# A decoder layer on one core: keys and exponentials turned by 32x32-block DMAs and VectorE transposes instead of TensorE

## The chip, the core and the metric

The kernel runs on one NeuronCore of a Trainium2 chip. The metric is the device time of one execution in microseconds; a comparison takes the median of several executions. The kernel before takes 1527.0 us (three runs: 1527.0, 1528.57, 1527.0).

## The reference

One post-norm decoder layer on 4 sequences of 512 tokens with 512 features: gated slot attention with 16 heads, a cross attention on a context of 4 x 512 x 256, and a quantized feed-forward of width 2048. Cut to what matters here:

```python
q, k = heads(x @ Wq, 64), heads(x @ Wk, 64)
v, s = heads(x @ Wv, 64), clip(heads(x @ Ws, 64), -32, 32)
z = cumlogsumexp(s, axis=time)
# hk_t = hk_(t-1) * exp(z_(t-1) - z_t) + k_t outer exp(s_t - z_t) ; ok_t = q_t @ hk_t
# hv_t = hv_(t-1) * exp(z_(t-1) - z_t) + exp(s_t - z_t) outer v_t ; o_t = softmax(ok_t) @ hv_t
o = rmsnorm(o) * g_norm_weight * silu(x @ Wg)
x = layernorm(x + o @ Wo)
x = layernorm(x + x @ softmax((ctx @ xWq + bq) @ (ctx @ xWk + bk).T))
x = layernorm(x + h_bitlinear(silu(bitlinear(x, w_gate)) * bitlinear(x, w_up), w_down))
```

The recurrences over time are computed in four chunks of 128 tokens. A chunk's state is the sum over its tokens of k outer exp(s); this sum is a matmul that needs k and exp(s) with **tokens on the partitions**, while the projections deliver them with features on the partitions and tokens along the row. So both have to be transposed, and that is what the change is about.

## The kernel before, in words

**Steps.** `PAIRS` lists 32 pairs (pair of heads, sequence). One attention step works on one pair: two heads side by side on 128 partitions, 512 tokens along the row. Step n runs the tail of pair n (states, sums, ok, softmax, weights, values), the projections of pair n+1 (`q`, `k`, `s`, `vg0` to `vg3`) and the output projection of pair n-1 (`turn_o`, `y`). All large matmuls are three passes (high x high, low x high, high x low) at lines 453, 456 and 459.

**The order of the work** is written out by hand in the tuples `ALONE` (steps 0 to 20) and `STEP` (from step 21); every engine walks the same list and picks its share, so a place in the tuple is a place in each engine's queue. Stages in `OF_NEXT` belong to pair n+1. The stage `tern` is a piece of preparing the ternary feed-forward weights: its first 24 tasks take sums of absolute values (ScalarE), the last 24 round (ScalarE) and clip and store (GpSimd, lines 1385 and 1388, semaphore `w3_made`). From step 22 on, cross attention is put between the stages by `PLACES` (one table per sequence: stage name and place number), then come a seam (`SEAM`) and the feed-forward in units of 128 features (`UNIT`). `HOLD` says for how many later requests a PSUM bank is taken to be busy, and so which bank comes next.

**The two transposes.** In the stage `keys` TensorE transposes KT (keys, 3 chunks of 128x128, line 500) and ET (exponentials, 4 chunks, line 504) against the identity into two PSUM banks; ScalarE copies them to Kt and Et (lines 814 and 819); the next step's first stage, `states`, multiplies Kt by Et (line 522). KT is written by ScalarE in stage `k` (line 799) and ET in stage `s` (line 802, the exponential). Kt and Et have one buffer each; Et of pair n is also read by `ok` (line 541) and `sums` (line 529) of step n.

**The DMA queue of SyncE (SP)** issues the weights: `pieces` is their order, two raw buffers `RAW` take turns, and before each piece SP waits until the buffer's former content was used (`left_raw`: for weights the low half made by GpSimd, line 1377; for feed-forward weights `w3_abs` or `w3_made`). Nothing overtakes on that queue. It also loads x into Y (line 1468) ahead of the first feed-forward weights.

**Head and tail.** SP issues the first pieces one after the other: x, Wq, x, x, x, Wk. At the end, the 16 `down` products of the last token tile go into one bank of 512 columns (line 717); VectorE adds it to Y (line 1312), takes moments (line 1315), GpSimd takes the root (line 1423), VectorE normalises (line 1322), and SP stores.

Of the kernel before, what the change touches and what calls it, by code (L numbers as in the profile page):

```python
# [35 lines left out]

class Queue:
# [5 lines left out]
    def wait_ge(self, sem, value):  # L43
        if value > self.passed.get(sem.name, 0):
# [6 lines left out]
         "y", "scores", "weights", "vg2", "load_x", "values", "keys", "tern", "vg3")  # L51
STEP = ("states", "q", "k", "tern", "load_x", "ok", "sums", "turn_o", "s", "turn_ok", "vg0", "turn_w", "tern", "vg1",
        "y", "vg2", "scores", "weights", "load_x", "values", "keys", "tern", "vg3")
OF_NEXT = ("q", "k", "s", "vg0", "vg1", "vg2", "vg3", "scores", "keys")


def step_order(n, tasks):

    terns = loads = 0
    for stage in ALONE if n < 21 else STEP:  # L60
        m = n + 1 if stage in OF_NEXT else n - 1 if stage in ("turn_o", "y") else n
        if stage == "tern":
            terns += 1
            if n and terns in ((2,) if n + 1 in LAST else (1, 2, 3)):
                for t in tasks[:1]:
                    yield stage, t
                del tasks[:1]
        elif stage == "load_x":
            loads += 1
            if n == 0:  # L70
                yield stage, loads + 1
        elif 0 <= m < STEPS:
            yield stage, m
# [26 lines left out]

PLACED = [stage for stage in STEP if stage not in ("scores", "sums", "load_x", "tern")]


def attention_order():

    for stage in OF_NEXT:
        yield stage, 0
    tasks = list(range(52))
    for n in range(STEPS - 1):
# [6 lines left out]
SEAM = (("states", 31), ("turn_o", 30), ("sums", 31), ("ok", 31), ("y", 30), ("turn_ok", 31), ("unit", 0), ("unit",  # L116
        1), ("turn_w", 31), ("unit", 2), ("weights", 31), ("unit", 3), ("values", 31), ("unit", 4), ("turn_o", 31),
# [6 lines left out]
def seam_order():  # L124

    for p, item in enumerate(SEAM):
        if item and item[0] == "unit":
            yield from ffn_place(item[1])
        elif item:
# [6 lines left out]
    dict(ctx=396, centre=402, n1=406, qk=407, qk_out=409, x101=414, x101_out=415, energy=417, energy_out=418,  # L136
         x123=419, att_scale=419, x123_out=420, att01=422, att01_out=424, att23=425, att23_out=426, xm0=430,
# [6 lines left out]
    dict(ctx=474, centre=474, n1=476, qk=477, qk_out=478, x101=479, x101_out=481, energy=481, energy_out=482,  # L144
         att_scale=483, att01=486, x123=487, x123_out=488, att01_out=488, att23=488, att23_out=489, xm0=491,
         xm0_out=492, xm1=493, xm1_out=494, xm2=495, xm2_out=496, xm3=497, xm3_out=498, x_round0=513, x_made0=514,
         x_round1=514, x_made1=515, x_turned=516, x_turned_out=517),
    dict(ctx=499, qk=502, qk_out=504, centre=518, n1=520, energy=522, energy_out=523, x101=524, att_scale=524,
# [19 lines left out]
def beside(place):  # L168
# [6 lines left out]
        38), ("low", 2), ("turn_q_out", 32), ("had2_out", 24), ("round", 29), ("high", 2), ("gs", 0), ("add", 35),  # L175
        ("had1", 4), ("normal", 37), ("turn_q", 31), ("had2", 23), ("down", 33), ("silu", 0))
# [4 lines left out]
HOLD = (("o", 12), ("en", 11), ("y", 7), ("vg", 9), ("xm", 11), ("gate", 7), ("up", 8), ("h1", 7), ("h2", 8), ("down",  # L181
        11), ("hq", 6), ("xt", 11), ("q", 5), ("k", 9), ("s", 9), ("sc", 13), ("wt", 7), ("ok", 12), ("okt", 8), ("w",
        6), ("ot", 10), ("kt", 4), ("et", 6), ("hk", 7), ("hv", 9), ("att", 12), ("x1", 11), ("qk", 11), ("spread",
# [27 lines left out]
vec_made hk_zero  # L211
x_hi x_lo_v x_lo_g w_hi w_lo_v w_lo_g wo_scaled w3_abs w3_sum w3_total w3_mean w3_round w3_clip w3_made
proj_q proj_k proj_s proj_vg q_evac k_evac s_clip e_exp v_evac g_tanh u_made
z_scan z_recip k_turned e_turned kt_evac et_evac scores a_masked hk_mm hv_mm hk_evac hv_evac hk_add hv_add
# [10 lines left out]
def build(nc, x, xT, Wq, Wk, Wv, Wg, Ws, Wo, gw, cT, xWqT, xbq, xWkT, xbk, wgT, wuT, wdT, cst, out):  # L225
    with ExitStack() as top:
# [143 lines left out]

        weight_no = {key: i + 1 for i, key in enumerate(key for key, _, _ in pieces if key[0] not in "xF")}
# [55 lines left out]
        def tensor(engine):  # L427
# [62 lines left out]
            def attend(stage, n):  # L490
                par = n % 2
                if stage == "keys":
                    bk = take(("kt", n), (S["kt_evac"], n + 1))
                    be = take(("et", n), (S["et_evac"], n + 1))
# [6 lines left out]
                    mm.then_inc(S["k_turned"], 1)  # L501
# [3 lines left out]
                    mm.then_inc(S["e_turned"], 1)  # L505
# [11 lines left out]
                elif stage == "states":  # L517
                    bh = take(("hk", n), (S["hk_evac"], n + 1), (S["hk_add"], 2 * n + 2))
                    pe.wait_ge(S["kt_evac"], n + 1)
                    pe.wait_ge(S["et_evac"], n + 1)  # L520
# [182 lines left out]
            def ffn_tile(stage, i):  # L703
# [8 lines left out]
                elif stage == "down":  # L712
                    bk = take(("down", i), (S["ffn_add"], i + 1))
                    pe.wait_ge(S["w3_in2"], 16 * 4)
                    for j in range(16):
                        pe.wait_ge(S[f"hq_evac{j // 8}"], i + 1)
                        mm = engine.matmul(bk[:], HT[:, j, :], WD[:, j, :], start=j == 0, stop=j == 15)  # L717
                    mm.then_inc(S["down"], 1)
# [30 lines left out]
        def scalar(engine):  # L749
# [19 lines left out]
            def ternary(t):  # L769
# [10 lines left out]
                elif what == "made":  # L780
# [4 lines left out]
                    act.wait_ge(S["vec_made"], 2)  # L785
# [3 lines left out]
            def attention(stage, n):  # L789
# [5 lines left out]
                elif stage == "k":  # L795
                    act.wait_ge(S["proj_k"], n + 1)
                    act.wait_ge(S["scores"], 2 * n)
                    act.wait_ge(S["e_turned"], n)
# [787 lines left out]
```

## Time and profile before

| | |
|---|---|
| median of three runs | 1527.0 us |
| the profiled execution, its own time | 1525.28 us |
| its span, first to last instruction | 1523.4 us |
| TensorE busy (PE) | 1488.2 us, 98% |
| VectorE busy (DVE) | 1032.0 us, 68% |
| ScalarE busy (ACT) | 653.9 us, 43% |
| GpSimd busy (POOL) | 432.0 us, 28% |
| DMA packets | 108016, 121.17 MB |

The table is read with two cautions. A busy TensorE is a row of matmuls that overlap: what one costs is the distance from its start to the start of the next, not its duration. And the busy share of another engine is an average over stages in which it is idle and stages in which everything waits for it.

### The profile page before, as it was taken

What the parts mean: (1) busy time and instruction counts of PE and PEld (TensorE: products, weight loads), DVE (VectorE), ACT (ScalarE), POOL (GpSimd) and SP (SyncE); (2) the same over time, 40 slices, a digit from 0 to 9 for tenths busy, and PEclk for the clock granted to TensorE, in tenths of its full rate; (3) what the DMA queues carried; (4) which work ended last, traced back from release to release, by engine and by line L of the source; (5) the groups of instructions that cost most, each with busy time, mean ns of one, the idle gap of its engine ahead of it and who ended that gap; (6) DMA issues with size and microseconds to landing.
All of it is one profiled execution on the core that took longest, in us unless ns stands there. A gap on an engine that the chain in (4) does not pass through costs nothing.

```text
span 1523.4 us, 24179 instructions
## 1 busy us (share of the span) xinstructions
PE 1488.2 (98%) x9536; PEld 1207.2 (79%) x9570; DVE 1032.0 (68%) x1990; ACT 653.9 (43%) x1249; POOL 432.0 (28%) x282
## 2 busy tenths in 40 slices
PE   8999999999999999999999999999999898999998
PEld 6888888888888888888888888878878655666675
DVE  5666665566556666665666577777787776877788
ACT  5333333333323333333443333424243357677775
POOL 0211011110214344433454423122331333333320
PEclk9999999999999999999999999999999999999999
DMA  4511111120102121222223211101110315344552
GB/s 154 180 52 67 42 49 56 56 66 33 63 15 79 62 88 65 83 70 70 84 80 101 87 28 54 49 22 42 52 41 26 111 70 176 122 132 136 155 170 93
DMA packets 108016, 121.17 MB, mean 80 GB/s; under 512 B 5376, under 2 KB 75136, under 8 KB 107904
## 3 DMA queue, kind: packets, MB, share of 16 engines
q1 hardware_dynamic: 104448, 113.33, 23.5%
q10 hardware_dynamic: 3456, 6.29, 1.1%
q8 instruction: 77, 1.26, 0.3%
q14 instruction: 35, 0.29, 0.1%
HBM read 92.34 MB, written 27.26 MB: 79 GB/s over the span
## 4 chain that ended last, share of the span: by engine, by line
PE 92%; DVE 5%; issue 2%; ACT 1%; DMA 0%; POOL 0%; POOLq 0%; SPq 0%; DVEq 0%; ACTq 0%
PE bank L453 19%; PE bank L459 18%; PE bank L456 18%; PE bank L682 6%; PE bank L579 4%; PE bank L697 4%; PE bank L717 3%; PE bank L541 2%; PE bank L514 2%; PE bank L587 2%; PE bank L565 2%; PE bank L536 1%; PE bank L522 1%; PE bank L529 1%; PE bank L573 1%
## 5 line engine op out<-in xcount | busy, mean ns | idle before, releaser
L453 PE MATMUL bank<-Wh,X 128*128 128x512 f32 x512 | 210.5, 411 | 0.1
L459 PE MATMUL bank<-Wh,X 128*128 128x512 f32 x512 | 201.0, 393 | 0.0
L456 PE MATMUL bank<-Wl,X 128*128 128x512 f32 x512 | 199.8, 390 | 0.0
L808 ACT ACTIVATE V<-bank 128x256 f32<-128x256 f32 x128 | 49.0, 383 | 315.5 <-PE bank L459 315.5
L453 PE MATMUL bank<-X,Wh 128*128 128x512 f32 x384 | 157.2, 409 | 7.6 <-ACT Wh L763 5.9
L1395 POOL TENSOR_TENSOR sm<-sm,half 128x8 f32<-128x8 f32 x32 | 52.8, 1649 | 387.3 <-DVE sm L1109 387.2
L1377 POOL TENSOR_TENSOR Wl<-RAW,Wh 128x512 fp32r<-128x512 f32 (+1 forms) x65 | 112.3, 1737 | 136.5 <-ACT Wh L763 136.5
L456 PE MATMUL bank<-X,Wh 128*128 128x512 f32 x384 | 151.0, 393 | 0.0
L459 PE MATMUL bank<-X,Wl 128*128 128x512 f32 x384 | 150.8, 393 | 0.0
L1418 POOL TENSOR_TENSOR LO<-M,HI 128x512 fp32r<-128x512 f32 x64 | 81.8, 1278 | 165.5 <-PE bank L691 106.0
L682 PE MATMUL bank<-XT,W 128*128 128x512 bf16 x492 | 118.1, 381 | 4.2 <-ACT XI L881 2.3
L1045 DVE SCALAR_TENSOR_TENSOR U<-U,bank 128x256 f32<-128x256 f32 x128 | 51.6, 404 | 100.9 <-ACT U L810 100.9
L459 PEld LDWEIGHTS bank<-Wh,X 128*128 128x128 f32 x512 | 96.1, 188 | 21.6
L453 PEld LDWEIGHTS bank<-Wh,X 128*128 128x128 f32 x512 | 96.3, 188 | 19.3 <-ACT Kt L814 0.4
L456 PEld LDWEIGHTS bank<-Wl,X 128*128 128x128 f32 x512 | 96.6, 189 | 17.2
L1043 DVE RECIPROCAL ZT<-ZT 128x512 f32<-128x512 f32 x32 | 107.3, 3353 | 1.1
L1385 POOL TENSOR_SCALAR RAW<-RAW 128x1024 f32<-128x1024 f32 x24 | 87.1, 3629 | 62.7 <-ACT RAW L786 62.2
L453 PE MATMUL bank<-Woh,OTh 128*128 128x512 f32 x256 | 99.8, 390 | 0.0
L456 PE MATMUL bank<-Wol,OTh 128*128 128x512 f32 x256 | 99.6, 389 | 0.0
L459 PE MATMUL bank<-Woh,OTl 128*128 128x512 f32 x256 | 99.6, 389 | 0.0
L1080 DVE TENSOR_TENSOR OKM<-bank,ZT 128x512 f32<-128x512 f32 x32 | 22.1, 691 | 112.0 <-PE bank L541 111.9
L682 PEld LDWEIGHTS bank<-XT,W 128*128 128x128 bf16 x512 | 48.8, 98 | 56.5 <-issue 8.5
(207 smaller groups left out, 3312.3 us busy)
## 6 DMA issues: line engine op xcount, KB each, us to landing
z_scratch<-EV SPq DMA_DIRECT2D x64, 256.0 KB, 2.0
Z<-z_scratch SPq DMA_DIRECT2D x16, 1024.0 KB, 5.9
RAW<-wgT SPq DMA_DIRECT2D x16, 512.0 KB, 3.9
RAW<-wuT SPq DMA_DIRECT2D x16, 512.0 KB, 3.8
RAW<-wdT SPq DMA_DIRECT2D x16, 512.0 KB, 3.6
RAW<-Wo SPq DMA_DIRECT2D x14, 512.0 KB, 3.6
RAW<-Wv SPq DMA_DIRECT2D x26, 256.0 KB, 2.9
RAW<-Wg SPq DMA_DIRECT2D x26, 256.0 KB, 3.4
```

The source lines that it names most:

```text
L453: engine.matmul(o, lh(c), rh(c), start=c == 0, stop=False)
L456: engine.matmul(o, lh(c), rl(c), start=False, stop=False)
L459: last = engine.matmul(o, ll(c), rh(c), start=False, stop=c == n - 1)
L579: mm = engine.matmul(bo[h][:, 128 * i:128 * i + 128], AM[:, h, i, :], V[:, par, i, 128 * h:128 * h + 128], start=False, stop=i == 3)
L682: mm = engine.matmul(bk[:], w[:, c, 128 * j:128 * j + 128], XT[b % 3][:, c, :], start=c == 0, stop=c == 3)
L697: mm = engine.matmul(bh[:, 128 * c:128 * c + 128], Z[:, i % 2, 4 * q + c, :], C[:, 4, :], start=True, stop=True)
L1043: engine.reciprocal(ZT[:], ZT[:]).then_inc(S["z_recip"], 1)
L1045: engine.scalar_tensor_tensor(u, u, 1.0, bank("vg", n, i)[:, 256:512], ALU.add, ALU.mult).then_inc(S["u_made"], 1)
L1377: engine.tensor_tensor(lo, r, hi, ALU.subtract).then_inc(S["w_lo_g"], 1)
L1385: engine.tensor_scalar(r, r, MAGIC - 1.0, MAGIC + 1.0, ALU.max, ALU.min).then_inc(S["w3_clip"], 1)
L1395: engine.tensor_tensor(smv[:, 4, :], smv[:, 3, :], half[:, 0:8], ALU.pow).then_inc(S["o_rstd"], 1)
L1418: engine.tensor_tensor(LO[:, n % 2, :], M[n % 3], HI[:, n % 3, :], ALU.subtract).then_inc(S["h_lo"], 1)
```

## The change

1. From pair 1 on, KT and ET are transposed without TensorE. SP issues 16 DMAs for each: DMA (a, b) moves the 32x32 blocks at partitions 32a of every chunk to partitions 32b of Kt (or Et), block columns 32a. So the blocks stand at their transposed places, and one VectorE `transpose` over the whole tile then turns each block inside, in place. The new stages `turn_k` (after `vg1`) and `turn_e` (after `vg2` or `weights`) hold the two VectorE instructions. The stage `keys` remains for pair 0 alone, now ahead of `scores`.
2. SP issues a send after the pieces whose buffer is freed earlier in the order, and before those that are freed later.
3. `load_x` of the last two sequences: one in step 0 and one in step 1 (before: both in step 0), without the first `tern` of step 1. The loads of Y are issued behind the second send of exponentials.
4. Head: the load of Wq is issued by ScalarE. Tail: the last `down` product is made in two halves of 256 columns, in two banks; add and moments follow per half.
5. Tables: `HOLD`, some places of `PLACES` (sequences 0, 2 and 3), the order in `SEAM` (`ok` ahead of `sums`, `unit 1` behind `turn_w`) and in `UNIT` (`round` last, `high` ahead of `had2_out`).

```diff
-         "y", "scores", "weights", "vg2", "load_x", "values", "keys", "tern", "vg3")
+         "turn_k", "y", "scores", "weights", "vg2", "turn_e", "values", "tern", "vg3")
...
-    dict(ctx=474, centre=474, n1=476, qk=477, qk_out=478, x101=479, x101_out=481, energy=481, energy_out=482,
+    dict(ctx=474, centre=474, qk=474, qk_out=475, n1=476, x101=479, x101_out=481, energy=481, energy_out=482,
...
+        def sent(n):
+            return 16 * 16 * n
...
                 if stage == "keys":
+                    if n:
+                        return
...
+            def turn(stage, n):
+                if stage == "turn_k":
+                    dve.wait_ge(S["kt_in"], sent(n))
+                    k = Kt[:].rearrange("p i n -> p (i n)")
+                    engine.transpose(k, k).then_inc(S["kt_made"], 1)
+                else:
+                    dve.wait_ge(S["et_in"], sent(n))
+                    e = Et[:].rearrange("p i n -> p (i n)")
+                    engine.transpose(e, e).then_inc(S["et_made"], 1)
...
+            def send(stage, n):
+                if stage == "k":
+                    sp.wait_ge(S["k_evac"], n + 1)
+                    sp.wait_ge(S["hk_mm"], n)
+                    src, to, done = KT[:, 0:384].rearrange("p (i b c) -> p i b c", i=3, b=4), Kt, S["kt_in"]
+                else:
+                    sp.wait_ge(S["e_exp"], n + 1)
+                    sp.wait_ge(S["ok_sum"], n)
+                    sp.wait_ge(S["hv_mm"], n)
+                    src, to, done = ET[:, n % 2, :].rearrange("p (i b c) -> p i b c", i=4, b=4), Et, S["et_in"]
+                for a in range(4):
+                    for b in range(4):
+                        engine.dma_start(to[32 * b:32 * b + 32, :, 32 * a:32 * a + 32],
+                                         src[32 * a:32 * a + 32, :, b, :]).then_inc(done, 16)
...
+                buffer = where if where in (0, 1) else None
+                until = max(until, freed.get(held.get(buffer), -1))
+                while sends and sends[0][0] < until:
+                    send(*sends.pop(0)[1:])
...
+                        halves = (bk, take(("down", 16), (S["ffn_add"], 17)))
+                        for js, cols, bh in [(js, cols, bh) for js in (range(8), range(8, 16))
+                                             for cols, bh in zip(COLUMNS, halves)]:
```

**Order on TensorE in step 17, around `values` and `vg3`.** V, AM are the values and the masked weights, C holds the identity, Wh and X the weights and x of `vg3`. Before:

```order
L459 MATMUL bank5<-Wh,X 128x512
L579 MATMUL bank3<-V,AM 128x128 [waits a2_masked]
L579 MATMUL bank3<-V,AM 128x128 x3
L579 MATMUL bank6<-V,AM 128x128 [waits a2_masked]
L579 MATMUL bank6<-V,AM 128x128 x3
L500 MATMUL bank4<-C,KT 128x128 [waits e_exp,y_add]
L500 MATMUL bank4<-C,KT 128x128 x2
L504 MATMUL bank7<-C,ET 128x128 x4
L453 MATMUL bank1<-Wh,X 128x512
L456 MATMUL bank1<-Wl,X 128x512
```

and with the change:

```order
L468 MATMUL bank4<-Wh,X 128x512
L591 MATMUL bank1<-V,AM 128x128 [waits a2_masked]
L591 MATMUL bank1<-V,AM 128x128 x3
L591 MATMUL bank2<-V,AM 128x128 [waits a2_masked]
L591 MATMUL bank2<-V,AM 128x128 x3
L462 MATMUL bank6<-Wh,X 128x512 [waits y_add]
L465 MATMUL bank6<-Wl,X 128x512
```

The seven transposes are gone, and nothing stands in their place.

**Order on VectorE in the same step, from the end of `vg1` to `values`.** ZT is the running sum, U the gate, Y the output, AM the masked weights, OG the squares. Before:

```order
L1043 RECIPROCAL ZT<-ZT 128x512 [waits z_scan]
L1045 SCALAR_TENSOR_TENSOR U<-U,bank6 128x256 [waits g_tanh]
L1136 TENSOR_TENSOR Y<-Y,bank1 128x512 [waits y_add,y_mm]
L1136 TENSOR_TENSOR Y<-Y,bank3 128x512 [waits y_mm]
L1136 TENSOR_TENSOR Y<-Y,bank5 128x512 [waits y_mm]
L1136 TENSOR_TENSOR Y<-Y,bank4 128x512 [waits y_mm]
L1102 TENSOR_TENSOR AM<-bank7,C 128x512 [waits weights]
L1102 TENSOR_TENSOR AM<-bank1,C 128x512 [waits weights]
L1045 SCALAR_TENSOR_TENSOR U<-U,bank5 128x256 [waits g_tanh]
L1106 TENSOR_REDUCE sm<-OG 128x2x4 [waits o_square]
```

and with the change:

```order
L1081 RECIPROCAL ZT<-ZT 128x512 [waits z_scan]
L1083 SCALAR_TENSOR_TENSOR U<-U,bank1 128x256 [waits g_tanh]
L1055 STREAM_TRANSPOSE Kt<-Kt 128x384 [waits kt_in]
L1174 TENSOR_TENSOR Y<-Y,bank0 128x512 [waits y_add,y_mm]
L1174 TENSOR_TENSOR Y<-Y,bank2 128x512 [waits y_mm]
L1174 TENSOR_TENSOR Y<-Y,bank4 128x512 [waits y_mm]
L1174 TENSOR_TENSOR Y<-Y,bank6 128x512 [waits y_mm]
L1140 TENSOR_TENSOR AM<-bank7,C 128x512 [waits weights]
L1140 TENSOR_TENSOR AM<-bank0,C 128x512 [waits weights]
L1083 SCALAR_TENSOR_TENSOR U<-U,bank4 128x256 [waits g_tanh]
L1059 STREAM_TRANSPOSE Et<-Et 128x512 [waits et_in]
L1144 TENSOR_REDUCE sm<-OG 128x2x4 [waits o_square]
```

Two transposes are added, each with a wait for DMAs: one ahead of the four additions to Y, one ahead of the sum of squares.

**Order on SP's queue around steps 16 and 17.** RAW<-wuT is a piece of feed-forward weights. Before:

```order
L1505 DMA RAW<-wuT 128x1024 [waits w3_made] x3
L1499 DMA RAW<-Wo 128x2x512 [waits w3_made]
L1505 DMA RAW<-wuT 128x1024 [waits w3_made]
L1505 DMA RAW<-wuT 128x1024 [waits w_lo_g]
L1505 DMA RAW<-wuT 128x1024 [waits w3_made] x2
```

and with the change, from the sends of exponentials in step 16 to those in step 17:

```order
L1523 DMA Et<-ET 32x4x32 [waits hv_mm,ok_sum,e_exp]
L1523 DMA Et<-ET 32x4x32 x15
L1594 DMA RAW<-wuT 128x1024 [waits w3_made]
L1594 DMA RAW<-wuT 128x1024 [waits w_lo_g]
L1594 DMA RAW<-wuT 128x1024 [waits w3_made] x2
L1523 DMA Kt<-KT 32x3x32 [waits hk_mm,k_evac]
L1523 DMA Kt<-KT 32x3x32 x15
L1523 DMA Et<-ET 32x4x32 [waits hv_mm,ok_sum,e_exp]
L1523 DMA Et<-ET 32x4x32 x15
```

The 16 sends of keys stand behind a piece that waits for GpSimd, and the 16 sends of exponentials behind those.

## Rows read from the trace of the kernel before

**Rows 1.** The page: part 1, part 4.

```profile
PE 1488.2 (98%) x9536; PEld 1207.2 (79%) x9570; DVE 1032.0 (68%) x1990; ACT 653.9 (43%) x1249; POOL 432.0 (28%) x282
PE 92%; DVE 5%; issue 2%; ACT 1%; DMA 0%; POOL 0%; POOLq 0%; SPq 0%; DVEq 0%; ACTq 0%
```

**Rows 2.** Timeline of TensorE, one step: start, us, engine, line, operation, count.

```profile
616.93 1.95 PE L579 MATMUL bank<-V,AM 128*128 128x128 f32 x16
618.72 0.49 PE L500 MATMUL bank<-C,KT 128*128 128x128 f32 x3
619.04 0.60 PE L504 MATMUL bank<-C,ET 128*128 128x128 f32 x4
619.40 0.47 PE L453 MATMUL bank<-Wh,X 128*128 128x512 f32 x1
...
622.25 0.83 PE L522 MATMUL bank<-Et,Kt 128*128 128x128 f32 x6
...
657.38 0.83 PE L522 MATMUL bank<-Et,Kt 128*128 128x128 f32 x6
```

**Rows 3.** Waits of TensorE: for whom, us in total, times, longest.

```profile
PE bank L587 <- DVE OG L1118: 4.0, 1, 4.0
...
PE bank L579 <- DVE AM L1102: 2.1, 1, 2.1
...
PE bank L565 <- DVE U L1045: 1.9, 1, 1.9
...
PE bank L453 <- DVE AM L1053: 1.1, 1, 1.1
```

**Rows 4.** Windows: us, busy of PE, PEld, DVE, ACT, POOL, PEclk, DMA, GB/s.

```profile
1020.00:1030.00 10.00, 7.34 (x65) 6.56 (x64) 8.61 (x23) 4.67 (x7) 5.02 (x3) 0.83 0.09 28
...
1200.00:1220.00 20.00, 14.71 (x97) 10.08 (x97) 12.98 (x26) 8.31 (x14) 7.26 (x5) 0.94 0.00 1
```

**Rows 5.** Timeline of ScalarE, the step of rows 2.

```profile
629.13 0.58 ACT L799 ACTIVATE KT<-bank 128x512 f32<-128x512 f32 x1
...
634.67 0.63 ACT L802 ACTIVATE ET<-ET 128x512 f32<-128x512 f32 x1 [3.43 <-DVE ET L1031]
```

**Rows 6.** Timeline of GpSimd, the step of rows 2.

```profile
633.01 1.04 POOL L1388 TENSOR_SCALAR BW<-RAW 128x1024 bf16<-128x1024 f32 x1
```

**Rows 7.** Timeline of SP's queue: DMAs issued back to back.

```profile
42.94 3.82 SPq L1468 DMA_DIRECT2D Y<-x  x4
...
798.58 0.47 SPq L1474 DMA_DIRECT2D XI<-xWkT  x1
799.09 0.47 SPq L1455 DMA_DIRECT2D CTX<-cT  x1
```

**Rows 8.** The page, parts 3 and 6: queue, packets, MB, share; issues, median us to landing.

```profile
q1 hardware_dynamic: 104448, 113.33, 23.5%
...
z_scratch<-EV SPq DMA_DIRECT2D x64, 256.0 KB, 2.0
```

**Rows 9.** Timeline of VectorE, the step of rows 2.

```profile
645.68 2.47 DVE L1136 TENSOR_TENSOR Y<-Y,bank 128x512 f32<-128x512 f32 x4
648.64 1.29 DVE L1102 TENSOR_TENSOR AM<-bank,C 128x512 f32<-128x512 f32 x2 [0.50 <-PE bank L565]
652.96 0.42 DVE L1045 SCALAR_TENSOR_TENSOR U<-U,bank 128x256 f32<-128x256 f32 x1 [3.02 <-ACT U L810]
654.68 1.22 DVE L1106 TENSOR_REDUCE sm<-OG 128x8 f32<-128x1024 f32 x1 [1.30 <-ACT OG L840]
```

**Rows 10.** The chain that ended last, around 1005 to 1026 us: start, us, what.

```profile
1014.65 3.35 DVE ZT L1043
```

**Rows 11.** Timeline: TensorE before the first step, VectorE in the tail.

```profile
29.69 0.91 PE L522 MATMUL bank<-Et,Kt 128*128 128x128 f32 x6 [0.78 <-ACT Et L819]
...
1517.85 0.75 DVE L1312 SCALAR_TENSOR_TENSOR Y<-bank,fs,Y 128x512 f32<-128x512 f32 x1 [1.78 <-PE bank L717]
1518.64 0.69 DVE L1315 BATCH_NORM_STATS2 st<-Y 128x6 f32<-128x512 f32 x1
```

More of the change, by code:

```diff
@@ L50 @@
 ALONE = ("states", "q", "tern", "k", "load_x", "ok", "sums", "s", "turn_ok", "turn_o", "vg0", "tern", "turn_w", "vg1",
-         "y", "scores", "weights", "vg2", "load_x", "values", "keys", "tern", "vg3")
-STEP = ("states", "q", "k", "tern", "load_x", "ok", "sums", "turn_o", "s", "turn_ok", "vg0", "turn_w", "tern", "vg1",
-        "y", "vg2", "scores", "weights", "load_x", "values", "keys", "tern", "vg3")
-OF_NEXT = ("q", "k", "s", "vg0", "vg1", "vg2", "vg3", "scores", "keys")
+         "turn_k", "y", "scores", "weights", "vg2", "turn_e", "values", "tern", "vg3")
+STEP = ("states", "q", "tern", "k", "load_x", "ok", "sums", "turn_o", "s", "turn_ok", "vg0", "tern", "turn_w", "vg1",
+        "y", "turn_k", "vg2", "scores", "weights", "turn_e", "values", "tern", "vg3")
+OF_NEXT = ("q", "k", "s", "vg0", "vg1", "vg2", "vg3", "keys", "scores", "turn_k", "turn_e")
 def step_order(n, tasks):
@@ L69, in step_order @@
             loads += 1
-            if n == 0:
-                yield stage, loads + 1
+            if n < 2 and loads == 1:
+                yield stage, n + 2
         elif 0 <= m < STEPS:
@@ L97, in raw_tasks @@
     yield STEPS - 1, ("WO", LOADS - 1)
-PLACED = [stage for stage in STEP if stage not in ("scores", "sums", "load_x", "tern")]
+PLACED = [stage for stage in STEP if stage not in ("scores", "sums", "load_x", "tern", "turn_k")]
 def attention_order():
-    for stage in OF_NEXT:
+    for stage in OF_NEXT[:9]:
         yield stage, 0
@@ L1327, in attention @@
                     project(stage, n)
+                elif stage in ("turn_k", "turn_e"):
+                    turn(stage, n)
                 else:
@@ L1484, in sync @@
                     placed.add(2)
+                if key == ("Q", 0):
+                    held[where] = key
+                    continue
                 buffer = {"am0": "am", "am1": "am", "og0": "og", "og1": "og"}.get(where, where)
@@ L1508, in sync @@
                                      wd[kind][:, :, 128 * hp:128 * hp + 128]).then_inc(done, 16)
+            for _, stage, n in sends:
+                send(stage, n)
             sp.wait_ge(S["ctx_lo_g"], 2)
```

122 lines of the change are left out of this document (78 added, 44 removed).

## The prediction

> **What bounds the kernel now.** I read the page's engine shares first, then the chain that ended last, then the waits of TensorE, then timelines of one step. TensorE is busy 98% of the span and holds 92% of the chain [rows 1]; so a TensorE instruction removed shortens the kernel by its start-to-start distance, where nothing new is waited for. One step runs from 622.25 to 657.38, 35.13 us [rows 2], with no TensorE wait inside it. What TensorE does wait for is a handful of single places [rows 3]; 4.0, 2.1 and 1.9 us of it lie in the stretch where cross attention and the seam are mixed in, and behind two of them the granted clock falls for a while [rows 4]. VectorE's 5% of the chain [rows 1] lies there too: around 1005 to 1026 us VectorE itself sets the pace, for example with a 3.35 us reciprocal [rows 10].
>
> **The change part by part.**
>
> *Transposes on TensorE.* The last value product starts a run at 616.93; the first transpose follows at 618.72, and `vg3` begins at 619.40 [rows 2]. Seven transposes cost 619.40 - 618.72 = 0.68 us, though their durations add up to more (they overlap). They go in 31 of 32 steps: 31 x 0.68 = **21.1 us**. The two ScalarE copies behind them go as well, worth nothing (ScalarE is 43% busy [rows 1]).
>
> *Keys, in their place.* In the step of rows 2 KT is ready at 629.13 + 0.58 = 629.71 [rows 5]. But the sends stand behind a piece that waits for GpSimd, which is done at 633.01 + 1.04 = 634.05 [rows 6]; with that piece's own issue (0.47 us [rows 7]) the sends begin at 634.5. No row shows a 32x32-block DMA. Nearest are plain DMAs issued back to back: 798.58 to 799.09, 0.51 us apart [rows 7]; the dearest in a row are the 1 MB loads of Y, 3.82 / 4 = 0.96 us each [rows 7]. A block DMA moves 12 or 16 KB, so I take 0.51 and keep 0.96 for the range. 16 x 0.51 = 8.2 us: issued by 642.7, landed by 644.7 with the 2.0 us of the 256 KB transfers [rows 8]. VectorE comes to `turn_k` just ahead of the additions to Y, at 645.68 [rows 9]: in time by 1 us.
>
> *Exponentials.* ET is ready at 634.67 + 0.63 = 635.3 [rows 5], earlier than the queue: issue 642.7 to 650.9, landed 652.9. VectorE comes to `turn_e` after the gate of `vg2`, 652.96 + 0.42 = 653.4 [rows 9]; in time by half a microsecond. TensorE needs the result at 657.38 - 0.68 = 656.7 [rows 2].
>
> *The VectorE transposes.* No row shows one. A 128x256 operation takes 0.42 us, a 128x512 addition 2.47 / 4 = 0.62 us [rows 9], and the dearest 128x512 operation 3.35 us [rows 10]. I take 0.55 (384 columns) and 0.65 (512 columns), near the plain operations. `turn_k` shifts the additions to Y from 645.68 and ends them at about 648.7, when VectorE waits for the weights anyway (0.50 us of idle, masks from 648.64); `turn_e` falls into 1.30 us of idle ahead of 654.68 [rows 9]. The masked weights are done by 650.0, `values` starts at about 652. So in plain steps both cost nothing; the cover is VectorE's idle time. At 3.35 us each they would cost 3 us a step.
>
> The Trainium skill (VectorE: DVE Perf Modes, The three transpose paths) gives 311 ns for a 128x128 VectorE transpose in bf16, an estimate of 0.93 and 1.24 us for 3 and 4 chunks; the sum below would be 0.8 us longer by it.
>
> *Where VectorE sets the pace.* Two chains lead to the waits of 2.1 and 1.9 us [rows 3]. There TensorE's 0.68 us only lengthens the wait, and `turn_k` (0.55) lies in the chain: 2 x 1.23 = **+2.5 us**. Below: 0; above: one new wait of the longest kind.
>
> *SP's queue.* The sends take 16.3 of 35 us. The weight loads behind them are late by 8 us each time, but two raw buffers and a whole step stand between load and use; I cost that at nothing. If the cover fails it shows as ScalarE waiting for a DMA.
>
> *Order of x loads, keys ahead of scores.* The wait of 1.1 us in step 0 [rows 3] comes from a VectorE mask behind the squares, with two x loads rounded just before; with one of them in the next step it goes: **-1.1**. Before the first step TensorE waits 0.78 us for the copy of Et [rows 11]; `scores` now stands between: **-0.8**. Late next are the sends of pair 1, with 10 us to spare.
>
> *Head and tail.* Wq's load is issued one place (0.47 us [rows 7]) earlier: between 0 and -0.5, taken **-0.2**. At the end, addition and moments of 0.75 and 0.69 us over 512 columns [rows 11] become halves, the first beside TensorE; 0.42 us for 256 columns [rows 9] leaves 0.6 to gain, less a little for twice the matmuls: **-0.5**, bounds 0 and -0.7.
>
> *Tables* (`PLACES`, `HOLD`, `SEAM`, `UNIT`): unknown sign. Best case, the three waits of rows 3 that lie there go (8.0 us) with their clock losses, (1 - 0.83) x 10 = 1.7 and (1 - 0.94) x 20 = 1.2 us [rows 4]: -10.9. Worst case, two more like the longest, 2 x (4.0 + 1.7) = +11.4. Taken 0, as nothing favours a side.
>
> *Sum*, against the profiled execution's own 1525.28 us: 1525.28 - 21.1 + 2.5 - 1.1 - 0.8 - 0.2 - 0.5 = 1504.1. The median of the runs is 1527.0, 1.7 above that execution; so **1505.8 us**.
>
> **The rivals.**
>
> *Slower: the queue sets the step.* The last block must land and be turned by 656.7. From 634.5, with 2.0 for landing and 0.65 for the turn, 32 issues have 19.5 us: 0.61 us each. Beyond it every step whose sends wait behind GpSimd pays 32 times the excess; by the order these are 5 steps with three rounding tasks and 9 that change weights ahead of the long cross steps, 14 in all. At 0.70 us it is 14 x 2.9 = 41 us: 1547. It decides at about 0.66 us, where the loss eats the 21 us. For it: the 0.96 of Y's loads. Against it: those are 1 MB each and fill the queues; every smaller one is at about 0.5.
>
> *Slower: the packets set it.* 128-byte runs mean 16 x 96 packets for keys and 16 x 128 for exponentials, 96 and 128 per DMA engine. The mean packet took 0.235 x 16 x 1523.4 / 104448 = 0.055 us [rows 8], at some 1085 bytes: 5.3 and 7.0 us, under the 8.2 of the issues. If each took double, 0.11, the two need 24.6 us instead of 19.5: 14 x 5.1 = 71 us, 1577. The Trainium skill has such a rule (DMA: Bandwidth & Descriptors, Specifications): below 512 bytes the engine reads, modifies and writes. No row here shows what that costs; a transfer between SBUF places with such runs is not in this trace.
>
> *New waits in the cross stretch*, the worst case of the tables: 1505.8 + 11.4 = 1517. For it: VectorE is the fullest there and gets two more instructions a step, each with a wait that holds all behind it.
>
> *The old waits go*, the best case: 1505.8 - 10.9 = 1495. For it: two PSUM banks are free in each step.
>
> *No change*: the saved 0.68 us is only waited elsewhere, if landings come late by just that: 1526. Against it: TensorE has no wait in the plain steps.
>
> **How the numbers follow.** Forecast 0.62 (its own range 1500 to 1511, from the bounds of head, tail, VectorE and half a new wait), old waits go 0.08, new waits 0.14, no change 0.05, the queue 0.08, the packets 0.03. Faster by more than 0.2% (3 us, about what a measurement of this kernel can tell): 0.62 + 0.08 + 0.14 = 0.84; within 0.2%: 0.05; slower: 0.11. The range takes in both cases of the tables with a margin of 2 us for a run against a run: 1493 to 1519; left out are 0.16.
>
> **What would show it.** Right: steps of 34.45 us in the plain part; seven transposes left in all on TensorE; issues of block DMAs about 0.5 us apart; VectorE transposes of 0.4 to 0.7 us with no TensorE wait at the `states` products; the waits in step 0 and before the first step gone. Wrong: a wait of `states` for VectorE's transposes, repeated every step (the queue or the packets); VectorE waiting long for the DMAs at `turn_k`, then TensorE for masks; ScalarE waiting for weight loads; or more idle time between 1000 and 1260 us than the 8 us of rows 3.

## The result and the profile after

The changed kernel takes **1557.3 us** (median of four runs, 1555.3 to 1557.7) against 1527.0: a ratio of 1.020, interval 1.019 to 1.021. The forecast was 1505.8 with a range of 1493 to 1519; the change made the kernel slower, in the way of the rival "the queue sets the step". All rows of the changed kernel below come from its profiled execution of 1557.0 us, with a span of 1555.0.

The page of the changed kernel, part 1 and the two rows of part 4, to be held against [rows 1]:

```profile
PE 1487.1 (96%) x9369; PEld 1194.8 (77%) x9369; DVE 1066.3 (69%) x2054; ACT 625.1 (40%) x1187; POOL 432.4 (28%) x282
PE 57%; SPq 20%; POOL 8%; DVE 5%; DMA 4%; issue 4%; ACT 2%; ACTq 0%; POOLq 0%; DVEq 0%
SPq L1523 19%; PE bank L462 10%; PE bank L468 10%; PE bank L465 10%; PE bank L694 6%; PE bank L709 4%; PE bank L730 3%; POOL RAW L1437 3%; POOL Wl L1429 3%; PE bank L591 2%; DMA Et<-ET 1%; PE bank L577 1%; DMA RAW<-Wk 1%; PE bank L553 1%; PE bank L526 1%
```

TensorE held 92% of the chain that ended last and now holds 57%. SP's queue, at 0% before, holds 20%, nearly all of it line 1523, the block DMAs. GpSimd's 8% is mostly the rounding (L1437) and the low halves of the weights (L1429), behind which the sends stand. Step 16, from 595.03 to 631.80, is the one ahead of the step that the prediction worked through (17), and VectorE comes to the keys at the same place in it, 23.5 us after its start against 23.4. The timeline of SP's queue in it (start, time from the first issue's start to the last one's end, engine, line, operation, count):

```profile
607.67 0.38 SPq L1588 DMA_DIRECT2D RAW<-Wo  x1
608.15 10.21 SPq L1523 DMA_DIRECT2D Kt<-KT  x16
618.47 11.21 SPq L1523 DMA_DIRECT2D Et<-ET  x16
629.73 11.18 SPq L1594 DMA_DIRECT2D RAW<-wuT  x3
```

The sends begin 13.1 us after the step's start at 595.03, 0.9 us later than the prediction put them in its step. But 16 issues take 10.21 and 11.21 us, **0.64 and 0.70 us each, not 0.51**: the last leaves at 629.68, not 16.3 but 21.5 us after the first. The page's part 6 gives the landings (count, KB each, median us from issue to landing), 1.8 and 1.9 us, near the 2.0 of [rows 8]:

```profile
Kt<-KT SPq DMA_DIRECT2D x496, 12.0 KB, 1.8
Et<-ET SPq DMA_DIRECT2D x496, 16.0 KB, 1.9
```

VectorE in the same step (in brackets the idle time before an instruction, and who ended it), where [rows 9] had no such waits:

```profile
619.59 0.58 DVE L1055 STREAM_TRANSPOSE Kt<-Kt 128x384 f32<-128x384 f32 x1 [1.05 <-DMA Kt<-KT]
620.10 2.44 DVE L1174 TENSOR_TENSOR Y<-Y,bank 128x512 f32<-128x512 f32 x4
...
630.94 0.71 DVE L1059 STREAM_TRANSPOSE Et<-Et 128x512 f32<-128x512 f32 x1 [3.53 <-DMA Et<-ET]
```

and TensorE, its only two waits in that step, to be held against [rows 2], where there was none:

```profile
595.03 0.83 PE L534 MATMUL bank<-Et,Kt 128*128 128x128 f32 x6
...
621.49 1.16 PE L577 MATMUL bank<-WT,ET 64*128 64x128 f32 x16 [0.99 <-DVE Y L1174]
...
631.80 0.91 PE L534 MATMUL bank<-Et,Kt 128*128 128x128 f32 x6 [1.02 <-DVE Et L1059]
```

The keys come 1.05 us late and hold the four additions to Y, which hold the PSUM bank that the weights want; the exponentials come 3.53 us late and hold the states. The step takes 36.77 us instead of 35.13.

In step 17 itself, from 631.80, a second loss shows. Before, its first rounding task began 0.54 us after the step's start at 622.25:

```profile
622.79 3.63 POOL L1385 TENSOR_SCALAR RAW<-RAW 128x1024 f32<-128x1024 f32 x1
```

With the change the load that this task needs leaves SP only behind the sends of step 16, at 629.73. ScalarE waits 5.78 us for it, and everything behind it is late:

```profile
634.46 1.24 ACT L810 ACTIVATE RAW<-RAW,half,ws 128x1024 f32<-128x1024 f32 x1 [5.78 <-DMA RAW<-wuT]
635.79 3.63 POOL L1437 TENSOR_SCALAR RAW<-RAW 128x1024 f32<-128x1024 f32 x1 [1.09 <-ACT RAW L810]
647.52 10.27 SPq L1523 DMA_DIRECT2D Kt<-KT  x16
```

The rounding begins 3.99 us into the step, the sends 15.7 us into it instead of the predicted 12.3, and the step takes 39.78 us. So the queue's delay comes round: late sends make the next loads late, these the rounding, and this the next sends.

The waits of TensorE over the whole run (for whom, us, times, longest) show the same two at the head of the list, ahead of everything in [rows 3]:

```profile
PE bank L534 <- DVE Et L1059: 22.2, 10, 4.9
PE bank L577 <- DVE Y L1174: 15.2, 10, 3.5
PE bank L462 <- ACT Wh L787: 6.2, 1, 6.2
```

The waits are not all that was lost: behind the longer ones the granted clock falls. At the start of step 1 TensorE waits 3.82 us. The sends of pair 1 begin at 37.15, 7.1 us into step 0, and their last issue ends at 60.02; 1.2 us of that are two loads of x between keys and exponentials. Step 0 had lasted 28.89 us before, so the exponentials come too late. And then:

```profile
62.16 0.91 PE L534 MATMUL bank<-Et,Kt 128*128 128x128 f32 x6 [3.82 <-DVE Et L1059]
...
64.25 0.63 PE L465 MATMUL bank<-X,Wh 128*128 128x512 f32 x1
64.68 0.63 PE L468 MATMUL bank<-X,Wl 128*128 128x512 f32 x1
...
66.77 0.40 PE L465 MATMUL bank<-X,Wh 128*128 128x512 f32 x1
```

The matmuls are 0.43 us apart there, against 0.23 in other steps: the lower of the two levels (1.2 GHz), until about 66.4. A window over the weight rounding, 440 to 940 us (columns as in [rows 4], `xN` are counts), before:

```profile
440.00:940.00 500.00, 499.47 (x3287) 425.02 (x3286) 316.24 (x577) 185.35 (x368) 209.46 (x106) 1.00 0.23 71
```

and after:

```profile
440.00:940.00 500.00, 466.53 (x2939) 389.83 (x2938) 301.12 (x549) 160.66 (x313) 199.41 (x98) 0.97 0.30 80
```

Before, TensorE is busy throughout at full clock; after, it idles and the mean clock is 0.97.

Step times, from the starts of the first `states` product of each step on TensorE's timeline; the second column has each step between the starts of 3 and 11, the third is (start of step 25 - start of step 11) / 14:

| kernel | steps 3 to 11 | mean of steps 11 to 25 | whole run, us |
|---|---|---|---|
| before | 35.13 | 35.15 | 1527.0 |
| changed | 34.3 to 34.6 | 37.84 | 1557.3 |

So the transposes' saving is there where no rounding task stands ahead of the sends, and lost where the rounding tasks and changes of weights do, in the 14 steps from 11 to 25.

### The profile page after: what moved, and what is told of

The parts are those of the page before. It is cut to its first block, busy times and chain, and to the rows that moved or that the text cites. A ratio compares the mean times of both kernels' runs of the same rounds, so it can differ in the third digit from the quotient of the medians.

```text
span 1555.0 us, 24857 instructions
## 1 busy us (share of the span) xinstructions
PE 1487.1 (96%) x9369; PEld 1194.8 (77%) x9369; DVE 1066.3 (69%) x2054; ACT 625.1 (40%) x1187; POOL 432.4 (28%) x282
## 2 busy tenths in 40 slices
DMA packets 234998, 135.49 MB, mean 87 GB/s; under 512 B 132352, under 2 KB 202112, under 8 KB 234880
## 4 chain that ended last, share of the span: by engine, by line
PE 57%; SPq 20%; POOL 8%; DVE 5%; DMA 4%; issue 4%; ACT 2%; ACTq 0%; POOLq 0%; DVEq 0%
SPq L1523 19%; PE bank L462 10%; PE bank L468 10%; PE bank L465 10%; PE bank L694 6%; PE bank L709 4%; PE bank L730 3%; POOL RAW L1437 3%; POOL Wl L1429 3%; PE bank L591 2%; DMA Et<-ET 1%; PE bank L577 1%; DMA RAW<-Wk 1%; PE bank L553 1%; PE bank L526 1%
## 5 line engine op out<-in xcount | busy, mean ns | idle before, releaser
L462 PE MATMUL bank<-X,Wh 128*128 128x512 f32 x384 | 160.1, 417 | 7.6 <-ACT Wh L787 6.2
L465 PE MATMUL bank<-X,Wh 128*128 128x512 f32 x384 | 153.7, 400 | 0.0
L1429 POOL TENSOR_TENSOR Wl<-RAW,Wh 128x512 fp32r<-128x512 f32 (+1 forms) x65 | 112.2, 1736 | 105.4 <-ACT Wh L787 105.4
L694 PE MATMUL bank<-XT,W 128*128 128x512 bf16 x512 | 123.5, 385 | 4.7 <-ACT XI L906 2.4
L462 PEld LDWEIGHTS bank<-Wh,X 128*128 128x128 f32 x512 | 96.8, 189 | 19.5 <-issue 0.6
L1437 POOL TENSOR_SCALAR RAW<-RAW 128x1024 f32<-128x1024 f32 x24 | 87.1, 3630 | 63.5 <-ACT RAW L810 63.1
L462 PEld LDWEIGHTS bank<-X,Wh 128*128 128x128 f32 x384 | 74.6, 194 | 25.8 <-ACT Wh L787 6.2
```

The lines of the kernel that those rows point to most:

```text
L462: engine.matmul(o, lh(c), rh(c), start=c == 0, stop=False)
L465: engine.matmul(o, lh(c), rl(c), start=False, stop=False)
L694: mm = engine.matmul(bk[:], w[:, c, 128 * j:128 * j + 128], XT[b % 3][:, c, :], start=c == 0, stop=c == 3)
L1429: engine.tensor_tensor(lo, r, hi, ALU.subtract).then_inc(S["w_lo_g"], 1)
L1437: engine.tensor_scalar(r, r, MAGIC - 1.0, MAGIC + 1.0, ALU.max, ALU.min).then_inc(S["w3_clip"], 1)
```

## The experiments

The page's row names and line numbers are those of each kernel; ratios are to the kernel before, run on the same chip at the same time.

**1. The price of an issue alone.** A kernel without the layer: groups of 16 DMAs of 32x3x32 blocks and of other shapes, one after the other.

> Nothing of the layer is computed here: groups of 16 DMAs issued back to back, each group after the one before has landed; the output is a copy of x. Queue theory (each issue from SP has a price of its own that hardly depends on what it moves): the groups of 32x3x32 and 32x4x32 blocks show 0.62 to 0.70 us per issue, as in the changed kernel, and a third of the packets (32x1x32) does not bring it under 0.55; landing about 2 us after the last issue. Packet theory (the 128-byte runs keep the DMA engines busy and hold the queue back): 32x1x32 falls to 0.45 or less, and 64- and 128-partition blocks of the same runs rise to 1.2 us or more. A third outcome: the price hangs on the form (32 partitions, SBUF as source); then 128-partition or plain 512-column transfers show 0.5 and the HBM source too. ScalarE's queue: the same as SP's by both theories; GpSimd's: open, 0.5 to 2 us.

Timeline rows of the DMA-issuing queues, each a group of 16; `t_k` blocks within SBUF, `t_plain` 32 rows of 512 columns within SBUF, `t_h2s` from HBM (blocks, then plain rows), `t_act` and `t_pool` blocks from the two other queues, `t_both` from two at once:

```profile
6.18 10.34 SPq L43 DMA_DIRECT2D t_k<-src  x16
...
76.12 10.07 SPq L43 DMA_DIRECT2D t_plain<-src  x16
87.64 7.43 SPq L43 DMA_DIRECT2D t_h2s<-x  x16
96.46 7.29 SPq L43 DMA_DIRECT2D t_h2s<-x  x16
105.40 10.39 ACTq L43 DMA_DIRECT2D t_act<-src  x16
...
128.95 8.76 POOL L43 DMA_DIRECT2D t_pool<-src  x16 [128.51 <-DMA t_act<-src]
138.93 10.68 SPq L43 DMA_DIRECT2D t_both_sp<-src  x16
138.93 10.39 ACTq L43 DMA_DIRECT2D t_both_act<-src  x16
```

10.34 / 16 = 0.65 us for a block DMA, 0.63 for a plain one within SBUF, 0.46 for either shape from HBM. The groups of other shapes in between took 10.0 to 11.0 us; one of them moves 384 runs of 128 bytes with each DMA, four times those of a block, in 10.74. Block shape, run length and packets hardly matter; both ends in SBUF does. The rows on which I had put my 0.51 [rows 7] are all loads from HBM.

**2. Fewer packets, same issues.** Only the first chunk of each tile moves, so a third and a quarter of the bytes; keys and exponentials are otherwise left as they were.

```diff
-                        engine.dma_start(to[32 * b:32 * b + 32, :, 32 * a:32 * a + 32],
-                                         src[32 * a:32 * a + 32, :, b, :]).then_inc(done, 16)
+                        engine.dma_start(to[32 * b:32 * b + 32, 0:1, 32 * a:32 * a + 32],
+                                         src[32 * a:32 * a + 32, 0:1, b, :]).then_inc(done, 16)
```

> The sends move only the first of the 3 (or 4) chunks, so Kt and Et are stale in the other chunks: the same 32 DMAs a step with 32 packets each in place of 96 and 128. Queue theory: issues stay at 0.55 to 0.69 us, the made steps stay late: 1535 to 1560 us. Packet theory: the landings come early and the kernel falls to 1500 to 1512 us.

One execution: 1547.6 us, span 1545.7, steps 11 to 25 at a mean of 37.35 us. In step 16 the two groups of 16 issues take 10.02 and 10.55 us. With 32 packets in place of 96 and 128 per DMA most of the loss is still there: not the packets.

**3. Sends ahead of the gated pieces.** A piece that a rounding task frees counts as freed two places later, one freed by the exponentials' weights one place later. So the sends of keys overtake the piece of the step's first rounding task, and those of exponentials the other.

```diff
-    freed["F", n // 27, n % 27 // 8, n % 27 % 8] = place
+    freed["F", n // 27, n % 27 // 8, n % 27 % 8] = place + 2
...
-    freed[key] = place
+    freed[key] = place + (key[0] == "S")
```

> Only SP's order differs: the sends of keys go ahead of the piece that waits for the step's first rounding task, and the sends of exponentials ahead of the piece that waits for the low half of S. Queue theory: in steps with three rounding tasks the sends begin at 7.5 us after the step's start in place of 12.3, and with 32 issues of 0.66 us the last block is turned 4 us earlier, just in time, so those steps return to about 34.4 us; steps that change weights stay about 1 to 2 us late. Together 1510 to 1535 us. Theory that the sends themselves (packets, or VectorE's waits wherever they stand) cost it: 1550 us or more.

1546.5 us, ratio 1.013 (1.0115 to 1.0145), outside both expectations. Most steps fell to between 34.4 and 36.2 us, but two took 49.6 and 48.3. In the first of them, SP's queue,

```profile
741.23 10.21 SPq L1523 DMA_DIRECT2D Kt<-KT  x16
751.55 11.67 SPq L1523 DMA_DIRECT2D Et<-ET  x16
763.26 0.59 SPq L1588 DMA_DIRECT2D RAW<-Wo  x1
```

and VectorE:

```profile
767.44 0.75 DVE L1030 TENSOR_SCALAR RAW<-RAW,gwc 128x1024 f32<-128x1024 f32 x1 [11.81 <-DMA RAW<-Wo]
```

The load of Wo now leaves behind 22 us of sends, VectorE waits 11.81 us for it in front of the masks, and TensorE 9.49 us for those. The queue is simply full at that place: whatever stands first there makes the other late.

**4. Keys by DMA, exponentials on TensorE.** `turn_e` becomes four TensorE transposes and a ScalarE copy behind the values; 16 sends a step remain.

> Keys go by DMA and VectorE, exponentials by TensorE and ScalarE as before: 16 issues a step in place of 32, four transposes back on TensorE (0.36 us a step). Queue theory: nothing is late any more, steps of 35.13 - 0.32 = 34.8 us: 1514 to 1522 us. If the loss came from the tables (places, banks, seam) and not from the queue: 1540 us or more.

1526.6 us, ratio 1.0001 (0.9991 to 1.001), slower than the 1514 to 1522 expected. Steps 2 to 11 take 34.81 us, a saving of 0.32 in each, as expected; steps 11 to 25 have a mean of 35.66, with one of 40.05. What remains is the wait at the weights for the additions to Y (7.7 us in 6 waits). The keys' own 16 issues still take 10.3 and 11.3 us in the two steps from 562.28 and 599.57, VectorE waits up to 3.46 us for them, and the saving is given back.

**5. Half the block DMAs.** Half of the blocks keep old contents; the count that VectorE waits for is halved with them.

```diff
-            return 16 * 16 * n
+            return 16 * 8 * n
...
-                    for b in range(4):
+                    for b in range(2):
```

> Only 8 of the 16 block DMAs of every tile are issued (b = 0 and 1), so half of Kt and Et keep old contents; all else as changed, both VectorE transposes included. Theory 'the issues on SP': 16 issues of 0.64 to 0.69 us are 10.7 us a step in place of 21.3, so from 634.5 the keys land at about 641.6 and the exponentials at about 647, both before VectorE comes to them; steps 12 to 25 fall to 34.3 to 34.8 us, the half-clock stretches behind the waits go, and the 38 us lost there and the 9 us not gained come back: 1505 to 1515. Rival 'the VectorE transposes and the moved orders': they are all still there, so the time stays above 1540.

**1498.9 us**, ratio 0.983 (0.981 to 0.984); steps 11 to 25 at 34.49; 6 us better than the best expected. SP's queue in step 16 issues 8 and 8 in 5.1 us each:

```profile
587.46 5.08 SPq L1523 DMA_DIRECT2D Kt<-KT  x8
592.65 5.09 SPq L1523 DMA_DIRECT2D Et<-ET  x8
```

All else of the change, VectorE's transposes included, is in this kernel. Halving the issues takes away 58 us. It halves the bytes and packets too, but run 2 took more of those away for 10 us: the loss lies in the issues.

**6. The same work with 10 issues.** One DMA writes each tile into a scratch in HBM, four read the blocks back to their transposed places.

```diff
+                blocks = z.rearrange("i (a p) (b c) -> b p i a c", a=4, b=4).rearrange("b p i a c -> b p (i a) c")
+                for b in range(4):
+                    engine.dma_start(to[32 * b:32 * b + 32].rearrange("p i (a c) -> p (i a) c", a=4),
+                                     blocks[b]).then_inc(done, 16)
...
+                engine.dma_start(zt[n % 2, 1].rearrange("i p n -> p i n"),
+                                 ET[:, n % 2, :].rearrange("p (i n) -> p i n", i=4)).then_inc(S["et_in"], 16)
```

> All of the computation; each tile goes through a scratch in HBM: one DMA writes it (SBUF as source), four read the blocks back to their transposed places (HBM as source). 10 issues a step in place of 32: 2 x 0.65 + 8 x 0.46 = 5.0 us, and each write has to land (about 2 us) before its reads. From 634.5 in the step of rows 2: writes issued by 635.9, keys read from about 637.5 and landed by 641.5, exponentials landed by 643.5; both before VectorE comes (645.7 and 653.4). Theory 'the issues on SP': plain steps of 34.3 to 34.8 us throughout, 1500 to 1515. Rival 'the way over DMA itself' (short runs, landing, VectorE's transposes, moved orders): the steps stay at 36 us or more behind the rounding tasks, above 1530.

**1498.7 us** (1498.5 to 1499.5), ratio 0.982 (0.981 to 0.984): the whole computation, faster than both kernels. SP's queue in step 17, which starts at 610.06:

```profile
623.07 0.43 SPq L1521 DMA_DIRECT2D t_scratch<-KT  x1
623.54 0.49 SPq L1525 DMA_DIRECT2D t_scratch<-ET  x1
627.46 1.86 SPq L1515 DMA_DIRECT2D Kt<-t_scratch  x4
629.43 2.00 SPq L1515 DMA_DIRECT2D Et<-t_scratch  x4
```

From first issue to last it is 8.4 us in place of 21.0 in step 17 of the changed kernel (21.5 in its step 16), the landing of the write (623.07 to 627.46) included, and the issues cost 0.43 to 0.50 each. The write lands later than I said (a median of 4.1 and 3.8 us, not 2), which the step has room for. The waits of TensorE and the window of the rounding stretch:

```profile
PE bank L463 <- ACT Wh L788: 6.3, 1, 6.3
...
PE bank L578 <- DVE Y L1175: 1.7, 2, 1.2
```

```profile
440.00:940.00 500.00, 498.25 (x3247) 422.01 (x3246) 338.18 (x625) 178.79 (x354) 216.98 (x110) 1.00 0.37 100
```

No wait for the states is left, two of 1.2 us or less for the additions, and the clock is at 1.00. The DMA share rose to 0.37 from 0.30, with more bytes and more packets than the changed kernel has (149.63 against 135.49 MB, 251857 against 234998 packets): more traffic, less time.

**7. The same, with `turn_k` next to `turn_e`,** behind the additions to Y:

```diff
-         "turn_k", "y", "scores", "weights", "vg2", "turn_e", "values", "tern", "vg3")
+         "y", "scores", "weights", "vg2", "turn_k", "turn_e", "values", "tern", "vg3")
...
```

> As the version over HBM, and the VectorE transpose of the keys stands next to that of the exponentials, behind the additions to Y and the gate, where TensorE's states first need it. If late keys ahead of the additions to Y still cost something there (the issue theory says little, since the keys are in time), this is 1 to 4 us faster than the version before; if nothing is late, the same within 1.5 us; the rival (VectorE's two transposes in a row late in the step delay the masks and the sum of squares) would make it 2 us or more slower.

1497.9 us (1497.6 to 1500.9), ratio 0.982: not to be told from run 6 in time. In the trace nearly every step from 2 to 25 takes 34.34 us, that of 35.79 in run 6 too.

**8. Everything else of the change.** Keys and exponentials back on TensorE, no sends; head, tail, x loads and tables as changed.

> No sends and no VectorE transposes: TensorE turns keys and exponentials for all pairs behind the values, with two ScalarE copies, as in the kernel before; head, tail, x loads, loads of Y and all tables as in the changed kernel. Theory 'the issues on SP': all of the loss lies in the sends, so this is the kernel before with the small terms of head, tail and step 0 (-1.8): 1520 to 1528, with steps of 35.1 us. Rival 'the moved orders': if the tables or the x loads cost the time, it stays at 1535 or more.

1527.0 us, ratio 1.0012 (1.0002 to 1.0021), steps of 35.13. The rest of the change together is worth nothing, within 0.2%.

**9. The block DMAs, with `turn_k` next to `turn_e`.** The edit of run 7 in the changed kernel.

> The changed kernel with one move: VectorE's transpose of the keys stands next to that of the exponentials, behind the additions to Y. Theory 'late keys hold the additions': TensorE's waits at the weights for the additions (15.2 us in 10 waits) go, with the half-clock stretches behind them: 1530 to 1545. Rival 'only the last block counts': the exponentials leave behind the keys on the same queue, so what the additions no longer wait for is waited for at the states, in the same steps: 1550 to 1560.

1555.4 us, ratio 1.019 (1.017 to 1.020). The wait at the weights went (15.2 us), and that at the states rose from 22.2 to 35.9 us in 14 waits. The rival I had set up is right: the order on VectorE decides where TensorE waits, not how long.

**10. Run 9 with the sends ahead of the first rounding task's piece,** the weights' loads left ahead of the exponentials (the first edit of run 3 alone).

> As the run before, and the sends of keys and exponentials stand ahead of the piece that the first rounding task frees (the piece counts as freed two places later), while the pieces freed by the exponentials' weights stay ahead of the sends of exponentials. The sends of keys then begin at about 630 in place of 634.5 in the step of rows 2: 26.7 us up to 656.7 for 32 issues of 0.64 to 0.69 (21.3 us) and 2.5 for landing and turn. Theory 'the queue in order': the steps fall to 34.3 to 35.6 and the two stretches of 48 to 50 us of the first such trial (a load of Wo late behind the sends) don't come: 1508 to 1525. Rival: what the sends gain, the weight loads behind them lose, on the same queue: 1540 or more.

1533.4 us, ratio 1.004 (1.003 to 1.006), between the two theories: the two long steps are gone, the mean of steps 11 to 25 is 36.25 us, and TensorE still waits 19.4 us at the states. Order alone gives back 22 of the 57 us between runs 9 and 7: where the sends start counts beside what they take.

**11. Two queues.** GpSimd issues the exponentials, SP the keys.

> The 16 sends of exponentials are issued by GpSimd at its place of that stage, the 16 sends of keys by SP as before; the same 32 DMAs, bytes and packets. Theory 'the issues on one queue': SP's share is 10.3 us a step, GpSimd's 16 x 0.55 = 8.8 us beside it, both done in time: 1500 to 1520, with GpSimd's rounding tasks some 9 us later in each step. Rival 'the DMA engines or the packets': the same transfers take as long from two queues, 1545 or more.

1610.8 us, ratio 1.056: a miss, and no test of what it was made for. GpSimd's timeline in one step:

```profile
700.75 1.74 POOL L1496 DMA_DIRECT2D Et<-ET  x3 [2.63 <-ACT ET L829]
705.48 1.64 POOL L1496 DMA_DIRECT2D Et<-ET  x3 [2.99 <-issue]
708.70 1.64 POOL L1496 DMA_DIRECT2D Et<-ET  x3 [1.57 <-issue]
...
718.00 0.55 POOL L1496 DMA_DIRECT2D Et<-ET  x1 [1.45 <-issue]
718.57 1.29 POOL L1429 TENSOR_TENSOR Wl<-RAW,Wh 128x512 fp32r<-128x512 f32 x1
719.95 3.62 POOL L1437 TENSOR_SCALAR RAW<-RAW 128x1024 f32<-128x1024 f32 x1
```

After every third issue GpSimd stands still for 1.45 to 2.99 us for nothing that the trace names: 16 issues take 17.8 us, not 8.8, and the weights' low halves, the rounding and the roots wait behind them. In run 1 that queue issued 16 DMAs of 96 packets without a pause; these have 128 each. Whether that is the reason was not tried, nor was ScalarE's queue as the second one, which issued beside SP without loss in run 1.

## Why the prediction was wrong

**The step that failed** is "I take 0.51 and keep 0.96 for the range" in *Keys, in their place*. The block DMA costs 0.64 to 0.70 us on SP (profile after, run 1), so the 32 of a step take 21.5 us, where the prediction had 16.3. With that its own sums turn round: in step 16 the keys, "in time by 1 us", come 1.05 us late; the exponentials, "in time by half a microsecond", come 3.53 us late. A second step failed with it, "I cost that at nothing" for the weight loads behind the sends: in step 17 ScalarE waits 5.78 us for one, and the sends start 3.5 us later than predicted. A forecast that stood on margins of 1 and 0.5 us out of 16 deserved far more than a chance of 0.08 for its rival, and the range should have followed the 0.96 that the text kept as a bound: it did not reach the queue's 1547. "Nearest" was judged by size; what mattered was that the transfer begins and ends in SBUF, and no row of before has that.

**The rival** named the mechanism, the 14 steps and the decision point of 0.66 us. At its 0.70 it gave a loss of 41 us and a time of 1547; the kernel took 1557. Against run 6, span 1496.6, the changed kernel's 1555.0 is 58.4 us longer: by the starts of the steps 45.5 of it lie in steps 11 to 25, 7.0 in steps 0 and 1, 3.1 between steps 25 and 31, 2.8 elsewhere. That 41 comes near 45.5 is partly luck: with the measured 21.4 us for 32 issues its rule gives 21.4 - 19.5 = 1.9 us a step, 27 in 14. What it lacked are the late loads that hold back the next rounding, steps 0 and 1, and the clock.

**Waits and clock.** The waits for Et and Y are 22.2 + 15.2 = 37.4 us against 1.7 in run 6: 35.7 of the 58.4. The mean granted clock over the span was 0.986 against 0.999: as an estimate (1 - 0.986) x 1555.0 = 21.8 us lost against 1.5, so 20.3. This is an upper bound. TensorE also idles at the low clock: in the windows of 7 us from 582, 821 and 937 us, all at 0.51, it was busy for 5.78, 4.28 and 5.25. And two executions of the changed kernel, at 0.983 and 0.989, took 1557.64 and 1557.68 us, where the estimate would put 9 us between them. So **up to a third of the loss is not waiting but slow matmuls behind the waits**, a cost that the prediction counted for the cross stretch [rows 4] and not for the steps; a sharper split is not shown.

**The packets** as a rival are out: a third and a quarter of the packets gave back 10 of 59 us (run 2), and run 6 has more of them. The Trainium skill (DMA: Bandwidth & Descriptors, Specifications) has the read-modify-write rule below 512 bytes; no run here shows a price for it: in run 1, 16 issues with 128-byte runs took 10.34 us with a median of 1.8 us to landing, 16 with 2 KB runs 10.07 and 2.0.

**Right, term by term**, where the queue is out of the way (runs 5 to 7):

- *The transposes on TensorE*: 0.79 us a step (35.13 - 34.34), where 0.68 was taken; over 31 steps 24.5 in place of 21.1. The prediction counted from the first transpose; from the start of the value products to `vg3` it was 616.93 to 619.40, 2.47 us, in [rows 2] and is 605.54 to 607.24, 1.70, in run 6.
- *VectorE's transposes*: 0.57 and 0.71 us against 0.55 and 0.65; free in plain steps, as said. The estimate from the Trainium skill's page (VectorE: DVE Perf Modes, The three transpose paths), 0.93 and 1.24, is higher than these rows; the measurement decides.
- *Where VectorE sets the pace*: +2.5 was not seen. From the states of step 25 to those of step 31 it took 1184.00 - 903.38 = 280.6 us before and 1160.21 - 885.60 = 274.6 in run 6: 6.0 saved, more than 6 x 0.79.
- *Order of x loads*: steps 0 and 1 took 65.4 us before and 62.5 in run 6; without two transposes' 1.6 that is 1.4 saved, for 1.1. In the changed kernel the same two steps took 69.5, because "10 us to spare" for the sends of pair 1 was wrong: its 32 issues and the two x loads between them took 22.9 us from 37.15, and TensorE waited 3.82 us.
- *SP's queue at nothing*: wrong with 32 issues, in the order of the change (step 17) and with the sends ahead of the loads (run 3). ScalarE's waits for loads of feed-forward weights are 46.5 us in the changed kernel and 13.6 before; the prediction named them as a sign that its cover fails. With half the issues (run 5) the sends of step 17 begin 13.1 us into it.
- *Head* and *the wait before the first step*: no gain shown; the first states start at 29.0 to 30.1 in all these kernels, at 29.69 before.
- *Tail*: -0.5 was right. Before, from the last `down` products to the start of the last normalisation, 1514.20 to 1520.40, are 6.20 us:

```profile
1514.20 3.61 PE L717 MATMUL bank<-W,HT 128*128 128x512 bf16 x16 [0.37 <-ACT HT L953]
...
1520.40 0.55 DVE L1322 TENSOR_SCALAR Y<-Y,mv,rs 128x512 f32<-128x512 f32 x1 [0.66 <-POOL rs L1423]
```

in run 7 they are 5.72:

```profile
1487.75 3.65 PE L741 MATMUL bank<-W,HT 128*128 128x256 bf16 x32 [0.37 <-ACT HT L979]
...
1493.47 0.55 DVE L1373 TENSOR_SCALAR Y<-Y,mv,rs 128x512 f32<-128x512 f32 x1 [0.66 <-POOL rs L1476]
```

- *Tables*: 0 was right, together with the rest (run 8).

So the forecast's picture of TensorE and VectorE held, that of SP's queue did not; with 10 issues in place of 32 the kernel takes 1498.7 us, 7 below the forecast, of which 0.11 x 31 + 2.5 = 5.9 are the two terms above.

## What to carry to other kernels

Count DMA issues as instructions on their queue, with a price from a row of the same kind of transfer, ends included; if no row has it, and the cover is a few per cent of the sum of issues, the chance belongs to the queue. Ask also what stands behind those issues: a load that leaves late can hold back the work that the next issues wait for. Many small DMAs within SBUF can be beaten by one write to HBM and a few reads that do the rearranging, although that moves more bytes, as it was here. And a wait on TensorE costs more than its length where the clock falls behind it: look at the granted clock of the stretch before pricing one that repeats.

## What the runs showed of the hardware

- The issue price goes by the ends: 0.63 to 0.70 us within SBUF, 0.46 to 0.50 from HBM to SBUF, 0.43 to 0.49 from SBUF to HBM for whole tiles (profile after, runs 1 and 6), nearly the same for 4 to 64 KB and for runs of 128 bytes or 2 KB.
- SP and ScalarE issue side by side without slowing each other (10.68 and 10.39 us for 16 each in run 1).
- GpSimd issued 16 DMAs of 96 packets in 8.76 us and 16 of 128 packets in 17.8, with a pause after every third; the cause is open.
- A write of 192 to 256 KB to HBM landed after a median of 4.1 and 3.8 us on this queue, where [rows 8] had 2.0 for one of 256 KB.
- After a wait of 3.82 us the matmuls ran at half the clock for a few us, 0.43 us apart in place of 0.23; over the changed kernel this cost, by the estimate above, at most 21.8 us.
